# GpSimd writes a scratch block behind each group of four gathers in layer 2, and waits for it

## What is computed

```python
def _graph_conv(x, W, edge_src, edge_dst, edge_weight, n_nodes):
    support = x @ W
    msg = support[edge_src] * edge_weight[:, None]
    return jax.ops.segment_sum(msg, edge_dst, num_segments=n_nodes)
...
h = _graph_conv(features, W1, edge_src, edge_dst, edge_weight, n)
out = _graph_conv(h, W2, edge_src, edge_dst, edge_weight, n)
...
xn = _layernorm(x, axis=-1)
x = x + gnn(xn, ...) + mix(xn[None], ...)[0]
x = x + ffn(_layernorm(x, axis=-1)[None], ...)[0]
```

## Time and profile before

| | us |
|---|---|
| median of 3 runs | 3555.98 (3555.76 to 3556.52) |
| profiled execution | 3530.59 |
| its span, first to last instruction | 3528.9 |
| layer 2, first gather to last | 1427.22 to 2604.56 |
| TensorE busy, share of the span | 2849.1, 81% |
| GpSimd busy, share of the span | 1914.3, 54% |
| mean granted TensorE clock | 0.911 |

### The profile page before, as it was taken

The page is one execution under the profiler, slowest core; times in us unless marked ns, Lnnn a source line. Parts: engine busy times, 40 slices in busy tenths (PEclk is TensorE's granted clock), DMA queues, the critical chain, the costliest instruction groups (busy, mean ns, idle before and its releaser), DMA issues.

```text
span 3528.9 us, 48884 instructions
## 1 busy us (share of the span) xinstructions
PE 2849.1 (81%) x14412; PEld 2020.4 (57%) x14413; DVE 1378.7 (39%) x3854; ACT 1369.9 (39%) x2993; POOL 1914.3 (54%) x2019
## 2 busy tenths in 40 slices
PE   1899989999999998788888888888877648989930
PEld 0566656656656665555555555555556637878820
DVE  8455545555454453322222222222225541111157
ACT  4687777777777772000000000000004323333322
POOL 2656656566555564566666666666644551222245
PEclk9999999999999999898988999898888869999975
DMA  6344434434444445655555555555532344444444
GB/s 217 123 155 161 158 120 158 156 123 160 157 146 128 156 157 174 211 165 158 159 165 160 163 163 161 161 159 165 159 95 90 107 135 128 140 152 124 133 149 123
DMA packets 268417, 527.05 MB, mean 149 GB/s; under 512 B 58824, under 2 KB 155087, under 8 KB 268097
## 3 DMA queue, kind: packets, MB, share of 16 engines
q0 software_dynamic: 88848, 240.99, 23.0%
q1 hardware_dynamic: 148256, 252.66, 21.9%
q10 hardware_dynamic: 31120, 31.04, 2.7%
HBM read 394.15 MB, written 131.79 MB: 149 GB/s over the span
## 4 chain that ended last, share of the span: by engine, by line
PE 60%; issue 13%; DVE 8%; another core or an unknown queue 6%; ACT 4%; DMA 4%; SPq 3%; DVEq 1%; ACTq 0%; POOL 0%; POOLq 0%
PE bank L1033 28%; PE bank L1021 11%; PE sums L1047 6%; PE bank L1262 4%; DMA pa<-ys_d 3%; PE bank L1123 3%; PE bank L1061 2%; PE bank L1250 2%; PE bank L1072 1%; PE sums L1002 1%; ACT build L830 1%; PE bank L1131 1%; ACT build L832 1%; ACT pa L953 1%
## 5 line engine op out<-in xcount | busy, mean ns | idle before, releaser
L725 POOL DMA_INDIRECT pa<-xn_d,srcs x816 | 782.5, 959 | 513.6 <-PE sums L1047 278.9
L1033 PE MATMUL bank<-t1s,pa 128*128 128x256 f32 x2450 | 650.5, 412 | 96.3 <-issue 93.0
L725 POOL DMA_INDIRECT pa<-h_d,srcs x544 | 521.8, 959 | 305.5 <-issue 146.9
L1033 PEld LDWEIGHTS bank<-t1s,pa 128*128 128x128 f32 x2450 | 491.5, 207 | 243.4 <-issue 178.3
L1033 PE MATMUL bank<-t0s,pa 128*128 128x256 f32 x2450 | 573.3, 392 | 37.7 <-DVE pa L1438 36.7
L1021 PE MATMUL bank<-build 128*128 128x343 f32 x1500 | 489.7, 470 | 112.2 <-DVE build L1420 61.0
L1033 PEld LDWEIGHTS bank<-t0s,pa 128*128 128x128 f32 x2450 | 470.9, 195 | 140.9 <-issue 73.6
L1438 DVE TENSOR_TENSOR pa<-bank,pa 128x343 f32 x750 | 361.4, 511 | 385.0 <-ACT pa L837 172.9
L1021 PEld LDWEIGHTS bank<-build 128*128 128x128 f32 x1500 | 274.9, 193 | 303.2 <-issue 196.7
L832 ACT ACTIVATE build<-build,ones 128x343 f32<-128x343 f32 x750 | 436.3, 582 | 24.4
L830 ACT ACTIVATE build<-build,tabs 128x343 f32<-128x343 f32 x750 | 424.9, 567 | 34.6 <-issue 27.4
(11 more groups left out here) (257 smaller groups left out, 2739.5 us busy)
## 6 DMA issues: line engine op xcount, KB each, us to landing
slab_d<-pa SPq DMA_DIRECT2D x175, 448.0 KB
pa<-slab_d SPq DMA_DIRECT2D x175, 448.0 KB
pa<-in_w ACTq DMA_DIRECT2D x32, 512.0 KB
pa<-in_w SPq DMA_DIRECT2D x32, 512.0 KB, 3.6
pa<-ys_d SPq DMA_DIRECT2D x109, 130.0 KB
pa<-xn_d,srcs POOLq DMA_INDIRECT x816
pa<-eo_d SPq DMA_DIRECT2D x49, 256.0 KB, 3.2
pa<-h_d,srcs POOLq DMA_INDIRECT x544
```

The costliest lines, as they stand in the source:

```text
L725: pool.indirect_dma_start(gath2[b * QT + j], None, table, bass.IndirectOffsetOnAxis(ap=srcs[:, n:n + 1], axis=0)).then_inc(s_g[b], 16)
L1033: ins = pe.matmul(app[i % 2][:, 0:D], slab3[:, s, :], table[:, s * D:(s + 1) * D], start=s == 0, stop=s == T - 1)
```

## The change

Behind the four gathers of each step of layer 2 GpSimd now writes zeros to a block of 500 columns by 128 partitions that nobody reads, which raises s_pc, and then waits until s_pc says that this block is written.

```diff
         gath2 = gath + [build[:, 6408 + k * D:6408 + (k + 1) * D] for k in range((RING2 - RING) * QT)]
+
+
+        spare = build[:, 8480:8980]
...
                     pool.indirect_dma_start(gath2[b * QT + j], None, table, bass.IndirectOffsetOnAxis(
                         ap=srcs[:, n:n + 1], axis=0)).then_inc(s_g[b], 16)
+                if layer:
+                    pool.memset(spare, 0.0).then_inc(s_pc, 1)
+                    pool.wait_ge(s_pc, s + 3)
```

## The result

The changed kernel takes 3565.5 us, median of 15 runs (3552.1 to 3571.5), beside 3556.4 us for the kernel before in 15 runs on the same chip (3548.3 to 3563.1). The ratio is 1.0022, interval [1.0012, 1.0032]: slower by some 8 us in 3560. The forecast was 3556.0, within 3540 to 3580. So the sum of the forecast was nearly right, and there is a small loss in it that the sum doesn't have. The experiments were about that loss, and about whether the near-zero came from the reserve.

A forecast was written before the change was run, and what follows sets the result against it. TensorE was taken to bound the kernel, with GpSimd waiting for it in layer 2. GpSimd's added 204 x 0.51 = 104 us fit into 147 us of reserve, so 0 was added to the median: 3556 us, range 3540 to 3580.

The forecast's parts named there:

- the sum of the forecast: Layer 2, GpSimd: 204 x 0.51 = 104 us more work against 147 us of reserve, so 0 on the path.
- the near-zero: Whole kernel: added time goes into GpSimd's existing pauses, so no change, 3556 us, chance 0.62.
- the reserve: GpSimd's waits for TensorE in layer 2: 0.72 us a group, 147 us in all, can take added work without loss.
- TensorE's slow stretches: Rival, layer 2: their shifting moves the time 10 to 20 us either way; chance 0.13 slower, 0.12 faster.

The follow-up runs named there:

- e1: Changed kernel with the 500-column memset kept, its wait moved from the next gather to the next memset; 3525.0 us, ratio 0.9997.
- e6: Changed kernel with a memset of one column, its wait put off to the next memset; 3554.5 us, ratio 1.0007.
- e9: Kernel before plus an always satisfied wait for s_pc behind the wait for s_hu, no memset; 3247.3 us, ratio 0.9999.
- e10: Changed kernel with its wait for s_pc moved behind the wait for s_hu, ahead of the same gather; 3448.6 us, ratio 1.0623.
- e12: Kernel before plus two always satisfied waits (s_pc, s_pool) behind each group of layer 2, no memset; 3245.7 us, ratio 0.9998.
- e5: Changed kernel with two memsets of one column behind each group, each waited for at once; 3568.0 us, ratio 1.0050.
- e4: Changed kernel with two memsets of 960 columns behind each group, each waited for; 3749.0 us, ratio 1.0643.
- e11: Kernel before with a ring of five groups in layer 2 instead of six; 3246.3 us, ratio 0.9996.
- e3: Changed kernel with the memset's block grown from 500 to 960 columns; 3560.4 us, ratio 1.0094.
- e7: Changed kernel without the memset, only an always satisfied wait for s_pc behind each group of layer 2; 3567.9 us, ratio 1.0050.

## What to carry to other kernels

Idle time of an engine is a reserve if it stands at a wait for the engine that sets the pace; count it per round, take off the gaps that belong to an instruction's price, and it says how much work fits in (here 0.72 us a group on the slower chips, and the loss beyond it came at full price). When a wait is added, look at the next instruction on that engine: if it has a wait already, one of the two moves into an instruction of its own (here the one written last), and a wait that is pending there costs 0.48 us more. In e1 and e6 the new wait was given to an instruction that had none, and nothing measurable was lost. To leave the wait that is more often pending on the instruction that does the work should help by the same price; no run here shows that it does, since e9 and e10 ran on a chip without such pauses. And such a reserve is read from one chip: another chip, 9% faster, had next to none of it.

## What the runs showed of the hardware

**A pending wait costs by where it stands.** Carried by the DMA_INDIRECT itself: 0.26 to 0.27 us from the signal to its start. In a separate instruction ahead of it: 0.74 to 0.75. Already satisfied: nothing where the sequencer is through with it long before (10 us or more in e9 and e12). But the gather starts no sooner than 0.71 to 0.72 us behind the separate instruction, and where that one can't run ahead, a satisfied wait costs too: in e5 the gap behind the memset is 0.60 instead of 0.27 us. The separate instruction's own record shows 17 ns, 43 with two waits in it (e12), so the price isn't in its row; it is in the idle time ahead of the next one.

**Two memsets in a row, each waiting for the one before, lose next to nothing.** 11.8 us over the 204 pairs, 0.06 us a pair, in e4 and in e5; from memset to gather it is 0.27 us. The group of e5:

```profile
L732 POOL MEMSET build<- 128x1 f32 x408 | 44.3, 109 | 11.8
```

**The chips differ by 9%, and not evenly.** For one and the same kernel on one core: 3556, 3522, 3553 and 3247 us. On the fast one layer 1 took 1176 us instead of 1300, and layer 2 1026 (e11) instead of 1174. The granted clock in layer 2 was 0.93 in e9 (1042 us), and 0.93 in the profile of the changed kernel too (1206 us); so the mean clock alone isn't the difference.

**TensorE's slow stretches.** They are the ones of the earlier trace rows, matmuls 0.7 or 1.4 us apart with "issue" ahead of them. In layer 2 of the kernel before they hold 181 us of TensorE's idle time. In e9 to e12 they are missing, but in e3 and e4, on a slower chip, they are too. The group of the dense units' matmuls in layer 2, before and in e3:

```profile
L1033 PE MATMUL bank<-t1s,pa 128*128 128x256 f32 x2364 | 629.6, 412 | 94.2 <-issue 91.6
```

```profile
L1039 PE MATMUL bank<-t1s,pa 128*128 128x256 f32 x2394 | 616.9, 415 | 0.0
```

So in layer 2 they aren't a mark of the chip: they are there in every kernel in which TensorE finds its gathers landed, and in none in which it waits for them. In layer 1 the chips do differ, some 25 to 30 us of such idle time on the slower ones and 1 us on the fast one, which is far less than the 124 us between 1300 and 1176. In these stretches s_hu is raised late, as the 8.8 us (median) from the matmul's recorded end to the gather in the pauses show, and now and then two raises lie within 0.1 us of each other. What these stretches are, and whether the late gathers of e7 bring on more of them, no run here settles.
